# Cross-attention's first pairs: key and query copies ahead of a norm, query products cut in halves

## The reference

```
x = x + xattn(layernorm(x), ctx, ctx)      # 16 heads of 16, 154 keys for each of 2 batches
    q = layernorm(x) @ Wq + bq;  k = ctx @ Wk + bk;  v = ctx @ Wv + bv
    softmax(q k / 4) v, heads side by side, @ Wo + bo
x = x + ffn(layernorm(x))                  # top 2 of 8 experts, gelu
```

## Time and profile before

| | us |
|---|---|
| median of 3 runs | 480.28 (479.03 to 480.95) |
| the profiled execution, its own time | 481.42 |
| its span, first to last instruction | 479.6 |
| TensorE busy | 405.4 |
| VectorE, ScalarE, GpSimd busy | 264.5, 227.5, 201.6 |
| first instruction of step 0 and of step 1 on TensorE (L1334) | about 53.2 and 68.6 |

### The profile page before, as it was taken

The page is one execution under the profiler, slowest core; times in us unless marked ns, Lnnn a source line. Parts: engine busy times, 40 slices in busy tenths (PEclk is TensorE's granted clock), DMA queues, the critical chain, the costliest instruction groups (busy, mean ns, idle before and its releaser), DMA issues.

```text
span 479.6 us, 8587 instructions
## 1 busy us (share of the span) xinstructions
PE 405.4 (85%) x2738; PEld 338.5 (71%) x2739; DVE 264.5 (55%) x592; ACT 227.5 (47%) x415; POOL 201.6 (42%) x183
## 2 busy tenths in 40 slices
PE   6956769999999998715789999999999999999920
PEld 2635647677667665512589999999999999999910
DVE  2768775474476112389485666564466868464300
ACT  1460654564555445150167466454466767554300
POOL 4753664753621432100515364454544444552221
PEclk9885779999999999855899999999999999999975
DMA  8336433624610111183453553552334662232220
GB/s 241 111 85 141 93 70 69 141 61 118 151 36 25 51 45 44 44 226 128 153 198 74 162 126 72 134 128 49 55 52 123 185 160 49 44 47 32 25 26 11
DMA packets 25718, 45.39 MB, mean 95 GB/s; under 512 B 6480, under 2 KB 19920, under 8 KB 22928
## 3 DMA queue, kind: packets, MB, share of 16 engines
q0 software_dynamic: 8448, 15.77, 18.4%
q1 hardware_dynamic: 13728, 26.32, 17.6%
q10 hardware_dynamic: 3504, 2.83, 1.9%
HBM read 31.52 MB, written 13.39 MB: 94 GB/s over the span
## 4 chain that ended last, share of the span: by engine, by line
PE 74%; DVE 10%; ACT 4%; DMA 3%; issue 2%; POOL 1%; ACTq 0%; POOLq 0%; DVEq 0%
PE ps_s L1617 22%; PE ps_t L1634 14%; PE ps_t L1637 7%; PE ps_s L1334 4%; PE ps_t L1382 3%; PE ps_c L1302 2%; PE ps_t L1379 2%; DVE mx L944 2%; DMA result<-big,rowtok 2%; PE ps_a L1404 2%; PE ps_a L1402 2%; ACT big L645 2%; PE ps_c L1599 2%; PE ps_a L1429 2%; PE ps_c L1404 2%
## 5 line engine op out<-in xcount | busy, mean ns | idle before, releaser
L1617 PE MATMUL ps_s<-xgT,KB 128*128 128x256 f32 x912 | 116.7, 284 | 3.0 <-DVE xgT L1220 3.0
L584 POOL DMA_INDIRECT result<-big,rowtok x38 | 67.7, 1780 | 112.8 <-DMA result<-big,rowtok 57.6
L1617 PEld LDWEIGHTS ps_s<-xgT,KB 128*128 128x128 f32 x912 | 111.5, 190 | 4.2 <-DVE xgT L1220 1.7
L944 DVE TENSOR_REDUCE mx<-ps_s 128x4 f32<-128x616 f32 x64 | 49.5, 796 | 37.0 <-PE ps_s L1334 36.9
L552 POOL DMA_INDIRECT big<-rows,gtok x38 | 42.8, 1125 | 42.9 <-DVE gtok L1197 23.7
L645 ACT ACTIVATE big<-ps_t 128x512 f32<-128x512 f32 x80 | 44.8, 594 | 25.2 <-PE ps_t L1379 16.7
L1634 PE MATMUL ps_t<-KB,HTb 128*128 x160 | 56.0, 394 | 0.0
L815 ACT ACTIVATE big<-ps_t,wrow 128x256 f32<-128x256 f32 x38 | 18.0, 474 | 69.9 <-PE ps_t L1637 66.1
L1634 PE MATMUL ps_t<-KB 128*128 x144 | 50.3, 394 | 0.0
L1263 DVE SCALAR_TENSOR_TENSOR big<-ps_t,wrow,big 128x256 f32<-128x256 f32 x38 | 18.3, 483 | 52.5 <-ACT big L815 44.8
L807 ACT ACTIVATE big<-ps_s 128x512 f32<-128x512 f32 x76 | 45.5, 599 | 0.0
(11 more groups left out here) (215 smaller groups left out, 702.8 us busy)
## 6 DMA issues: line engine op xcount, KB each, us to landing
VP<-in_wexp SPq DMA_DIRECT2D x8, 1024.0 KB, 5.8
big<-in_wexp SPq DMA_DIRECT2D x8, 1024.0 KB
qd<-big SPq DMA_DIRECT2D x28, 128.0 KB, 2.3
KB<-qd POOLq DMA_DIRECT2D x7, 512.0 KB, 5.3
result<-x SPq DMA_DIRECT2D x8, 256.0 KB, 3.2
rows<-xn SPq DMA_DIRECT2D x8, 256.0 KB, 3.4
KB<-qd POOLq DMA_DIRECT2D x7, 256.0 KB, 5.9
XS<-in_x ACTq DMA_DIRECT2D x1, 1024.0 KB, 5.4
```

Of the source, the lines that this page charges most:

```text
L584: pool.indirect_dma_start(out, bass.IndirectOffsetOnAxis(rowtok[:, u, h:h + 1], 0), ys[:, 2 * (u % 2) + h, :], None, compute_op=ALU.add).t ...
L944: dve.tensor_reduce(mx[:, i, :, 2 * k:2 * k + 2].rearrange("p a b -> p b a"), ps_s[n % 2][:, :, 0:2 * KEYS].rearrange("p b (h k) -> p b h ...
L1617: last = mm(ps_s[j // 4][:, j // 2 % 2, (j % 2) * PAIR:(j % 2 + 1) * PAIR], w1[:, w, k, j * P:(j + 1) * P], xgT[:, u % 2, a, k, :], start= ...
```

## The change

The computation stays the same; orders change on four engines.

- VectorE: the norm of pair 2 (L886) moves from ahead of the first queries' copies and all keys' work to behind the last copy of keys. `statistics1(3)` moves from between the maxima of pair 0 to behind the values, and `statistics1(4)` from between the maxima of pair 1 to behind `negatives(1)`.
- TensorE: the transposes of pair 2 move from ahead of the value products to behind the first two scores. `q_product(2)` is cut into two halves, one before score (0, 4) and one before (0, 5), instead of standing whole before (0, 3). The transposes of pair 3 move from before score (1, 3) to before (1, 5). `q_product(3)` is halved: the first half stands behind the last score of pair 1, the second in step 0 behind turned score 0.
- ScalarE: the two `ones` instructions of batch 0 are parted around `evac_xnT(2)`, `last_keys(0)` goes ahead of `evac_q(2)`, and `evac_q(3)` moves into step 0, behind exponential 0.
- GpSimd: `next_norm1(3)` goes behind `queries_read(2)` and `maxima_read(0)`.

The queues of SyncE, and of GpSimd apart from that one move, are unchanged.

```diff
@@ GpSimd
             low_queries(2)
-            next_norm1(3)
             queries_read(2)
             maxima_read(0)
+            next_norm1(3)
             low_queries(3)
             next_norm1(4)
@@ ScalarE
             evac_q(1)
+            ones(0, (0,))
             evac_xnT(2)
-            ones(0)
+            ones(0, (1,))
+            last_keys(0)
             evac_q(2)
-            last_keys(0)
             evac_maxima(0)
             evac_xnT(3)
-            evac_q(3)
             ones(1)
             evac_maxima(1)
@@ ScalarE, step(m)
                     exp(m, 0)
+                if m == 0:
+                    evac_q(3)
@@ VectorE
             for m, loaded in ((1, ld_x0), (2, ld_x1)):
                 dve.wait_ge(loaded, 16)
                 statistics1(m)
-            dve.wait_ge(rstd1_made, 3)
-            dve.wait_ge(xn_made, 4)
-            dve.wait_ge(xnT_psum, 1)
-            for i in range(2):
-                dve.tensor_scalar(xn[:, 0, i, :], xs[:, 4 + i, :], mv1[:, 0, i, 0:1], mv1[:, 0, i, 3:4],
-                                  ALU.subtract, ALU.mult).then_inc(xn_made, 1)
             dve.wait_ge(qf_made, 1)
...
             low_keys(0, range(4))
-            for n in range(4):
-                maxima(0, n)
-            statistics1(3)
-            for n in range(4, 8):
+            dve.wait_ge(rstd1_made, 3)
+            dve.wait_ge(xn_made, 4)
+            dve.wait_ge(xnT_psum, 1)
+            for i in range(2):
+                dve.tensor_scalar(xn[:, 0, i, :], xs[:, 4 + i, :], mv1[:, 0, i, 0:1], mv1[:, 0, i, 3:4],
+                                  ALU.subtract, ALU.mult).then_inc(xn_made, 1)
+            for n in range(8):
                 maxima(0, n)
             negatives(0)
             all_values()
-            for n in range(4):
+            statistics1(3)
+            for n in range(8):
                 maxima(1, n)
+            negatives(1)
             dve.wait_ge(ld_x2, 16)
             statistics1(4)
-            for n in range(4, 8):
-                maxima(1, n)
-            negatives(1)
@@ TensorE
-            def q_product(m):
-                pe.wait_ge(xnT_made, m + 1)
-                for g in range(GROUPS):
+            def q_product(m, gs=range(GROUPS)):
+                if 0 in gs:
+                    pe.wait_ge(xnT_made, m + 1)
+                for g in gs:
...
-                last.then_inc(q_psum, 1)
+                if GROUPS - 1 in gs:
+                    last.then_inc(q_psum, 1)
@@ TensorE
             q_product(1)
-            xn_transposes(2)
             pe.wait_ge(ld_v, 32)
             for b in range(B):
                 value_product(b)
-            for n in range(3):
+            for n in range(2):
                 scores(0, n)
-            q_product(2)
-            for n in range(3, 8):
+            xn_transposes(2)
+            for n in range(2, 4):
+                scores(0, n)
+            for g in range(GROUPS):
+                q_product(2, (g,))
+                scores(0, 4 + g)
+            for n in range(4 + GROUPS, 8):
                 scores(0, n)
             maxima_transposes(0)
-            for n in range(3):
+            for n in range(5):
                 scores(1, n)
             xn_transposes(3)
-            for n in range(3, 5):
-                scores(1, n)
-            q_product(3)
             for n in range(5, 8):
                 scores(1, n)
+            q_product(3, (0,))
             maxima_transposes(1)
@@ TensorE, step(m)
                     turned_scores(m, 0)
+                if m == 0:
+                    q_product(3, (1,))
```

More of the change, by code:

```diff
@@ L668, in first_queries, with ones @@
                     act.activation(QS[0:32, 0, 2 * r:2 * r + 2, :], qf[32 * r:32 * r + 32, :, :], ACT.Copy).then_inc(q0_high, 1)
-            def ones(b):
+            def ones(b, heads_of=(0, 1)):
                 act.wait_ge(own_made, 1)
-                for a in range(2):
+                for a in heads_of:
                     act.activation(KS[96:100, b, :, a * KEYS:(a + 1) * KEYS],
```

## The result

The changed kernel takes 482.75 us (median of 20 runs, 480.88 to 486.05) beside 480.65 for the kernel before: ratio 1.005, 95% interval 1.0033 to 1.0066. It is slower, by about 0.25 to 0.5%: the first interval lies clear of 1, the second just takes it in. The forecast was 480.3, with a range of 476.2 to 484.0. Some executions of a kernel take about 7 us longer than the rest (two of the 20 of the kernel before), and all ratios leave them out.

What follows compares the result with a forecast made beforehand. TensorE was taken to set the pace from step 2 on, handing earlier gains and losses on one to one. 4.6 us won in the filling and 4.7 lost in step 0 gave 480.3 us, range 476.2 to 484.0.

Steps and rivals of the forecast that it cites:

- the second rival: Step 0: the queue of pair 4's norm behind low_queries(3) decides; 7 us longer, 4.6 gained, 482.9 us; chance 20%.
- after that the same: Sign in the profile after: step 1 starts near 68.7, and everything behind it is as before.
- Up to the first maximum: Start of the filling, mainly VectorE: the first maximum starts at 26.4 instead of 27.95, bounds 24.6 and 28.6.
- The third rival: Filling: GpSimd blocks VectorE's copies one for one until 19.9, first maximum at 28.6, time 482.5 us; chance 7%.
- Maxima of pair 0: Filling, VectorE and TensorE: pair 0's maxima take 7.4 us in all, done at 33.8, clock mostly full.
- Maxima of pair 1: Filling: first maximum at 38.6, 2.6 us of waiting before the sixth, step 0 at 48.6, 4.6 us ahead.
- One sign that I had named for being wrong: Filling, GpSimd: the prediction is wrong if the read of pair 2 is quicker than 5.1 us.
- Step 0: First step: pair 4's transposes wait for GpSimd's norm until A + 9.4; the step lasts 20.1 us, 4.7 more.
- A: Instant at which the first scores of step 0 start: forecast 48.6, taken as 53.24 before.
- The mis-sized term: Step 0, pair 4's transposes to evac_q(4): 5.3 us, between 3.75 at full and 7.5 at half clock.
- The first: Rival: the filling's gain is kept, TensorE's clock full at pair 4's transposes or norm queue shorter; about 476.8 us; chance 31%.

Runs made afterwards that it cites:

- The early norm of pair 3: Changed kernel with statistics1(3) ahead of the values on VectorE and next_norm1(3) ahead of queries_read(2) on GpSimd: ratio 0.9954 to the kernel before.
- The exchange in GpSimd's queue: Changed kernel with next_norm1(4) ahead of low_queries(3) on GpSimd, nothing else altered: ratios 0.9899 and 0.9904 to the kernel before.
- the half product alone: Kernel before with only q_product(3) in halves and its second half and evac_q(3) in step 0: ratio 1.0114 to the kernel before.
- The filled step: Changed kernel with 18 unread matmuls on TensorE ahead of pair 4's transposes in step 0: ratio 0.9968 to the kernel before.

## Why the prediction was right

The forecast (no change, 480.3) was that 4.6 us are won in the filling and 4.7 lost in step 0. Measured by the profile they are 4.1 and 5.1, and the time is 1.3 to 2.4 us longer than before. The mechanism is as forecast: each of the two stages moved the way and nearly as far as given. The time is less well met than that. 482.75 lies at the edge of the forecast's own range (477.9 to 482.7) and next to the second rival's 482.9. The start of step 1 is 1.0 us later than before in both pairs of profiles taken in order (69.61 and 68.63, 68.95 and 67.96), and no term of the sum gives the rest of what the first comparison measured; "after that the same" isn't shown.

- **Up to the first maximum**: right in the sum (26.4 given, 25.98 measured), by luck in part, with terms that cancelled. The copies took 0.53 us each (2.13 for four), not 0.95, and ended at 16.6, not 18.3; bias, masks and L914 took 0.8 more than I carried over; the norm took the full 2.03 of my upper bound, not 1.4. The third rival, with copies blocked one for one until 19.9, didn't happen; only its full 2.0 for the norm did. The Trainium skill, "SBUF — State Buffer", section "Who interferes with whom", has the rule behind it: of a VectorE cast or tensor_scalar in a two-port mode and a GpSimd instruction the second to issue is blocked until the first ends. The trace again shows it in kind (the norm's 2.03 beside GpSimd's L452), and again not in full for the copies.
- **Maxima of pair 0**: 7.4 given, 7.7 measured (25.98 to 33.71). The clock wasn't full throughout: 0.81 from 24.45 to 27.36, and the first half product took 1.75 us, as at half clock, the second 1.03.
- **Maxima of pair 1**: first maximum 38.6 given, 38.62 measured; the wait before the sixth 2.6 given, 2.37 measured; step 0 at 48.6 given, 48.86 measured (49.2 where the last transposes end, which is how I had read it before). One sign that I had named for being wrong did come: the read of pair 2 was issued 4.7 us after its first store (34.07 to 38.76), not 5.1. The wait was there all the same, and only a little shorter. The early norm of pair 3 shows the cause of that wait: with it step 0 starts at 46.5.
- **Step 0**: transposes of pair 4 at A + 9.4 given, A + 9.17 measured; the standstill and its releaser are as described. The exchange in GpSimd's queue and the half product alone show the cause from both sides.
- **The mis-sized term**: from the transposes to `evac_q(4)` I gave 5.3 us, between 3.75 at full and 7.5 at half clock. It was 6.2 (58.03 to 64.22). So the end of step 0 was at 69.61, not 68.7. The filled step puts the clock's part of step 0 at 2.4 us, where I had allowed 1.55 (5.3 less 3.75).
- **Rivals**: the second names the right mechanism and direction. Its price for step 0 (7 us longer) was too high, beside 4.7 in the forecast and 5.1 measured, so that its total of 482.9 agrees with the measured 482.75 only by luck (and 7 less 4.6 on top of 480.3 is 482.7). The first, with a full clock in step 0, is what the filled step shows: 0.997 there, where I gave 476.8 us (0.993).

What stays open: I had said that what the filling and the first step gain or lose is handed on to the end one to one, and the ratios don't show that. Ratios and the start of step 2 agree in the main in order, but not in size. With pair 4's norm first, step 2 starts 1.1 to 3.6 us earlier than in the profiles of the kernel before, 2.4 in the mean, and the gain is about 4.7 us; the half product alone is 2.4 to 3.4 us late and loses 5.5. The difference lies behind step 2, where the instructions are the same. One thing in the profiles goes with it. Step 4 takes 17.7 to 17.8 us in seven of the thirteen, with the clock at 0.91 from 124 to 142, and 16.2 in six, with the clock at 1.00. All four profiles with pair 4's norm first are among the six and both of the changed kernel among the seven, but the kernel before has one of each, and no experiment ties this stretch to the timing of the filling.

## What to carry to other kernels

When work is moved later to shorten one stage, read what each in-order queue has behind the instruction that waits for it: here half a product of 1 us moved into step 0 pulled a 1.3 us instruction on GpSimd after it, and behind that stood a norm of over 3 us for which TensorE had to wait in the same step. Ask of each stall that an edit removes which wait ends last next, and order the queue by who is waited for; three calls put elsewhere in two queues turned a loss of 0.3 to 0.5% into a gain of 1.1 to 1.7%. And price a standstill of TensorE twice, once for the wait and once for the work at half clock behind it: here 4.7 us of idling brought another 2.4.

## What the hardware showed that I had not expected

- 18 matmuls whose result nobody reads, 4.06 us of pure waste inside a wait, made the kernel 0.6 to 0.8% faster than without them (0.9968 against 1.005 and 1.0026), since the granted clock stayed at 1.00 where it had been 0.53.
- Queries made in step 0 are only just in time for step 1: with pair 4's norm first, GpSimd's read of pair 3's queries was issued at 59.33, and the score that wants it waited for it until 65.50. In the kernel before it was issued at 56.34 and nobody waited.
